# The last two tiles reach the router unnormed, their logits corrected afterwards; buffers and steps without a pair put in another order

## The reference

```python
x = x + memory_attention(layernorm(x))          # 8 kv heads; elu(q)+1 times M, over a denominator, then Wo
x = x + cross_attention(layernorm(x), ctx)      # below
x = x + router_ffn(layernorm(x))                # below
# cross_attention: 32 query heads in 4 groups, keys and values from concat(ctx, latents)
q = (latents @ Wq).reshape(b, q_len, 4, 8, 128)
attn = softmax(einsum('bqhgd,bkhd->bhgqk', q, k) * scale)
out = einsum('bhgqk,bkhd->bqhgd', attn, v).reshape(b, q_len, 4096) @ Wo
# router_ffn: 64 experts, 8 kept
logits = flat @ router_weight.T + router_bias
scores = softmax(logits)
topk_w, topk_idx = lax.top_k(scores, 8)
out = flat * topk_w.sum(-1) + w_dense @ expert_bias
```

## Time and profile before

| | before |
|---|---|
| median of 3 runs | 720.72 us (719.7 to 722.87) |
| the profiled execution's own time | 720.87 us |
| its span, first to last instruction | 719.1 us |
| PE busy | 692.9 us, 96% |
| DVE, ACT, POOL busy | 510.3, 349.5, 115.8 us |
| mean granted PE clock | 0.993 of full speed |

### The profile page before, as it was taken

How to read it: one execution, slowest core, us unless ns; L and a number is a source line. 1 busy time by engine, 2 the same in 40 slices (tenths; PEclk the granted TensorE clock), 3 DMA queues, 4 the chain that set the end, 5 groups by cost and what they waited for, 6 DMA issues and landing times.

```text
span 719.1 us, 10998 instructions
## 1 busy us (share of the span) xinstructions
PE 692.9 (96%) x3562; PEld 581.1 (81%) x3562; DVE 510.3 (71%) x1078; ACT 349.5 (49%) x1042; POOL 115.8 (16%) x121
## 2 busy tenths in 40 slices
PE   8999699999999998999999999999999999899995
PEld 6888588887887787888888888888888888688874
DVE  2764877678725878677677876767977566778876
ACT  4454655456244446344445643554645336555541
POOL 0175400000101332020120220210202000022410
PEclk9999999999999999999999999999999999999998
DMA  9888510001234456543242833423542404221101
GB/s 329 296 288 286 205 59 1 1 0 59 88 118 143 135 170 206 189 147 100 77 126 80 263 102 102 146 87 110 194 146 78 146 31 154 75 82 59 59 16 58
DMA packets 69997, 90.14 MB, mean 125 GB/s; under 512 B 4224, under 2 KB 47232, under 8 KB 69952
## 3 DMA queue, kind: packets, MB, share of 16 engines
q1 hardware_dynamic: 64160, 80.13, 34.2%
q10 hardware_dynamic: 5792, 9.44, 3.7%
HBM read 62.29 MB, written 27.26 MB: 125 GB/s over the span
## 4 chain that ended last, share of the span: by engine, by line
PE 83%; DVE 8%; DMA 2%; issue 2%; ACT 2%; POOL 1%; SPq 0%; POOLq 0%; ACTq 0%; DVEq 0%
PE bank L896 23%; PE bank L828 19%; PE bank L652 14%; PE bank L965 7%; PE bank L1014 5%; PE bank L798 5%; PE bank L991 4%; PE bank L643 1%; DMA raw<-in_L_attn_Wo 1%; PE bank L765 1%; DVE regA L1364 1%; PE bank L687 1%; PE bank L731 1%; DVE forms L1364 1%; DMA raw<-in_ctx 1%
## 5 line engine op out<-in xcount | busy, mean ns | idle before, releaser
L896 PE MATMUL bank<-regA,oT 128*128 128x512 f32 x768 | 180.6, 391 | 3.1 <-DVE oT L1364 3.1
L896 PEld LDWEIGHTS bank<-regA,oT 128*128 128x128 f32 x768 | 143.4, 188 | 33.3 <-DVE oT L1364 3.9
L1290 ACT ACTIVATE probs<-bank,negmax 128x128 f32<-128x128 f32 x256 | 90.1, 378 | 46.0 <-DVE negmax L1741 46.0
L828 PE MATMUL bank<-xnT,forms 128*128 128x512 f32 x384 | 97.2, 397 | 0.2
L828 PEld LDWEIGHTS bank<-xnT,forms 128*128 128x128 f32 x384 | 70.1, 188 | 15.2 <-DVE qbuf L1571 1.7
L828 PE MATMUL bank<-regC,forms 128*128 128x512 f32 x288 | 75.8, 401 | 2.4 <-DVE qbuf L1571 2.4
L1044 ACT CAST oT<-bank 128x512 fp32r<-128x512 f32 x64 | 37.6, 588 | 79.3 <-PE bank L1014 76.5
L1044 ACT CAST pT<-bank 128x512 fp32r<-128x512 f32 x64 | 34.7, 592 | 69.5 <-PE bank L991 69.5
L652 PE MATMUL bank<-regC,xnT 128*128 128x512 f32 x256 | 67.8, 396 | 0.0
L965 PEld LDWEIGHTS bank<-k_ring,qbuf 128*128 128x128 f32 x512 | 62.0, 191 | 2.5
L828 PEld LDWEIGHTS bank<-regC,forms 128*128 128x128 f32 x288 | 52.8, 190 | 12.9 <-DVE qbuf L1571 2.4
(11 more groups left out here) (151 smaller groups left out, 1072.0 us busy)
## 6 DMA issues: line engine op xcount, KB each, us to landing
q_dram<-qbuf SPq DMA_DIRECT2D x32, 512.0 KB, 3.0
qbuf<-q_dram SPq DMA_DIRECT2D x31, 512.0 KB, 4.5
raw<-in_L_attn_Wo SPq DMA_DIRECT2D x8, 1024.0 KB, 7.6
raw<-in_L_xattn_Wo SPq DMA_DIRECT2D x4, 2048.0 KB, 9.9
wq_raw<-in_L_xattn_Wq SPq DMA_DIRECT2D x16, 512.0 KB, 4.1
k_ring<-keys_dram SPq DMA_DIRECT2D x32, 128.0 KB, 3.6
v_raw<-vals_dram SPq DMA_DIRECT2D x64, 64.0 KB, 3.5
rawk<-in_L_xattn_Wv SPq DMA_DIRECT2D x4, 512.0 KB, 4.0
```

The source lines that it names most:

```text
L828: last = nc.tensor.matmul(k_bank[:, :], forms[:, p[1], a, i, c, :], right(b)[:, c, :], start=j == 0, stop=j == 5)
L896: last = nc.tensor.matmul(bank[7][:, :], oT[:, a, h, :], wo[:, b, h, :], start=h == 0 and i == 0, stop=h == GH - 1 and i == 2)
L1290: last = nc.scalar.activation(probs[:, bb, p, :], bank[bb][:, p * P:(p + 1) * P], ACT.Exp, bias=negmax[:, bb, p:p + 1], accum_out=rowsum[: ...
```

## The change

It has these parts:

- **Staging buffers.** `kv_slots` is turned round, so result 14 lies in `qneg` and result 15 in `kvout`. ACT's first exp then waits for result 14's write; DVE waits for result 15's only ahead of the first denominator sum.
- **End of the memory attention.** The transposes of latent tile 5 and DVE's and ACT's share in them move one step back; the split of the key weights (`wkv_high(1, ...)`, `wkv_low(1, ...)`) moves behind the last latent tile.
- **Last forms before the steps.** `summed_high` and `summed_low` of pair 5 move from ahead of step (0,0) into it.
- **Steps without a pair.** In (2,7) and (3,1) the last two heads of `project` come behind the transposes of the probabilities. At a group's first step ACT makes its last four `wo_high` ahead of the rounding of `oT`. In step (3,0) DVE makes two `wo_low` ahead of `oT` and two behind it, and POOL makes the last four.
- **Router.** A matrix of ones times the router's weights gives their sums once (`router_sums`, four matmuls in step (3,2)). Tiles 6 and 7 are transposed as raw residual; DVE corrects the logits by mean and rstd, kept by `keep_norm`. The last mix has its own bank, the tail's streams are reordered.

```diff
-        kv_slots = (qneg[:, :], qb[:, :], kvout[:, :])
+        kv_slots = (kvout[:, :], qb[:, :], qneg[:, :])
...
+        def mix_bank(e):
+            return bank[0] if e == NT - 1 else bank[2]
+
+        def rows_of(e):
+
+            return resid[:, e, :] if e >= NT - 2 else e_xn_of(e)
...
+            pool.wait_ge(form_lo, 4 * PAIRS)
+            nc.gpsimd.memset(ones, 1.0).then_inc(ones_set, 1)
+            for h in range(4, GH):
+                pool.wait_ge(wo_hi, GH * (KV - 1) + h + 1)
+                pool.wait_ge(wo_lo, GH * (KV - 1) + h)
+                nc.gpsimd.tensor_tensor(wo[:, 1, h, :], wo_raw[:, h, :], wo[:, 0, h, :].bitcast(F), ALU.subtract)\
+                    .then_inc(wo_lo, 1)
...
-                if output_in(i):
+                if output_in(i) and i != 2 * NT + 1:
                     latent_transposes(output_in(i) - 1)
+                if i == 2 * NT + 2:
+                    latent_transposes(output_in(i - 1) - 1)
...
             def expert_transposes(e):
-                pe.wait_ge(e_xn_ready, e + 1)
+                if e >= NT - 2:
+                    pe.wait_ge(proj_added, 8 * (KV - 1) + e + 2)
+                else:
+                    pe.wait_ge(e_xn_ready, e + 1)
...
+            def router_sums():
+
+                pe.wait_ge(routT_ready, 1)
+                pe.wait_ge(ones_set, 1)
+                for c in range(KC):
+                    nc.tensor.matmul(bank[3][:, NE:2 * NE], ones, routT[:, c, :], start=c == 0, stop=c == KC - 1)
...
+                divided = not pair and not (last_group and t >= 2) and t
+                front = range(GH - 2) if divided else range(GH)
                 if not first_step:
                     if t == 0:
                         project(g - 1, 7, True)
                     else:
-                        project(g, t - 1, False)
+                        project(g, t - 1, False, front)
...
+                elif divided:
+                    project(g, t - 1, False, range(GH - 2, GH))
...
+            expert_transposes(NT - 2)
             project(KV - 1, NT - 1, False)
-            expert_transposes(NT - 2)
+            expert_logits(NT - 2)
             expert_weights(NT - 3)
+            expert_transposes(NT - 1)
             expert_mix(NT - 3)
-            expert_logits(NT - 2)
-            expert_transposes(NT - 1)
             expert_logits(NT - 1)
...
-            act.wait_ge(kv_written[0], kv_count(0, 16))
+            act.wait_ge(kv_written[2], kv_count(2, 16))
...
             for p in range(LEAD + 1):
                 copy_1(p)
-                summed_high(p + 1, (p + 1) % 2)
+                if p < LEAD:
+                    summed_high(p + 1, (p + 1) % 2)
...
-                if t % 2 and has_pair(g, t + 2):
+                if first_step or t % 2 and has_pair(g, t + 2):
                     summed_high(pair + 1, slot)
...
+                    if s == 0:
+                        dve.wait_ge(kv_written[0], kv_count(0, 16))
...
             x_low(tr("latent", NT - 1), NT - 1)
+            wkv_low(1, wkv2, 3 * KC, 0)
...
+            def keep_norm(e):
+
+                r = e % 2
+                nc.vector.tensor_copy(top[:, r, 1, 1:2], meanvar[:, 0:1])
+                settled(nc.vector.tensor_scalar(top[:, r, 1, 2:3], rstd[:, 0:1], -1.0, None, ALU.mult))
+
...
+                if e == 0:
+                    nc.vector.tensor_copy(rout_sums, bank[3][:, NE:2 * NE])
+                if e < NT - 2:
+                    nc.vector.tensor_tensor(logits, bank[3][:, 0:NE], rout_b, ALU.add).then_inc(logits_saved, 1)
+                    dve.wait_ge(logits_saved, e + 1)
+                else:
+
+                    nc.vector.scalar_tensor_tensor(out=small[:, r, 4, :], in0=rout_sums, scalar=top[:, r, 1, 1:2],
+                                                   in1=bank[3][:, 0:NE], op0=ALU.mult, op1=ALU.subtract)\
+                        .then_inc(logits_saved, 1)
+                    dve.wait_ge(logits_saved, e + 1)
+                    settled(nc.vector.scalar_tensor_tensor(out=logits, in0=small[:, r, 4, :],
+                                                           scalar=top[:, r, 1, 2:3], in1=rout_b,
+                                                           op0=ALU.mult, op1=ALU.add))
...
-                if t % 2 and has_pair(g, t + 2):
+                if first_step or t % 2 and has_pair(g, t + 2):
                     summed_low(p + 1, slot)
...
                 if t == 0 and not first_step:
-                    for h in range(2 if p is not None else 0, 4):
+                    for h in range(2) if p is None else range(2, 4):
                         wo_low(g, h)
...
                 if t == 0 and not first_step:
-                    for h in range(4, GH):
+                    for h in range(2, 4) if p is None else range(4, GH):
                         wo_low(g, h)
```

More of the change, by code:

```diff
@@ L885, in _, with project @@
                 product_3(pair)
-            def project(g, t, release):
+            def project(g, t, release, heads=range(GH)):
                 n = 8 * g + t
-                pe.wait_ge(oT_lo, 2 * n + 2)
-                pe.wait_ge(proj_added, n + 1)
-                for h in range(GH):
+                if heads[0] == 0:
+                    pe.wait_ge(oT_lo, 2 * n + 2)
+                    pe.wait_ge(proj_added, n + 1)
+                for h in heads:
                     if t == 0:
@@ L1316, in step @@
                     high(pT[:, bb, 0, :], bank[bb][:, :]).then_inc(pT_hi, 1)
+                if t == 0 and not first_step:
+                    act.wait_ge(proj_done, 8 * g)
+                    for h in range(4, GH):
+                        wo_high(g, h)
                 for bb in range(2):
@@ L1821, in _ @@
                 step(KV - 1, t, True)
+            expert_rows(NT - 2)
+            keep_norm(NT - 2)
             add_mix(NT - 4)
@@ L1827, in _ @@
             expert_moments(NT - 1)
+            expert_max(NT - 2)
             expert_rows(NT - 1)
[L1829 removed]
+            keep_norm(NT - 1)
             add_mix(NT - 3)
```

46 lines of the change are left out of this document (21 added, 25 removed).

## The result

The changed kernel takes 735.77 us (median of 4 runs, 733.65 to 738.87) against 720.34 of before in the same runs: a ratio of 1.0205, 95% interval 1.0164 to 1.0246. It is 15 us slower, where 7.7 were forecast. The profiled execution took 735.96 us, with a span of 734.2.

The account below looks back on a forecast made before the run. PE's stream was taken to bound the kernel, busy 692.9 of 719.1 us. Terms summed to -4.7, giving 725.4 us; two clock falls (-3.0) made the forecast 728.4 us, range 720.0 to 731.5.

Parts of the forecast that it names:

- the latent value products hide it: End of the memory attention: the late key weights' split serves only the latent key products, so costs nothing; unhidden, 2.8 us.
- the clock fall at the first step: Behind the new wait for `qbuf` at the scores of (0,1): PE's clock falls, 1.5 us lost.
- End of the memory attention, +0.6: Tile 6's norm on DVE comes one operation earlier, PE waits less: 0.6 us gained, bounds +0.3 and +0.6.
- Pair 5, -1.6 and 1.5 of clock: Step (0,0): old wait and clock fall go, but `qbuf` loads late: 1.6 us lost, plus 1.5 for a new fall.
- `wo_low` on POOL, -5.2 and 1.5: Steps (3,0), (3,1): POOL's four subtractions delay the router's loads: 5.2 us lost, plus 1.5 for a clock fall.
- Heads in (2,7), +1.0: Step (2,7): heads 6 and 7 behind the transposes fill PE's idle 1.01 us ahead of L1014: 1.0 us gained.
- router: Step (3,2): four more f32 matmuls for the sums, partly filling small waits: 0.3 us lost, bounds 0 and -0.9.
- tail: Kernel's end: transposes fill a wait, the last mix skips DVE's add: 0.6 us gained, bounds +0.3 and +1.1.
- Staging buffers, +0.2: Memory steps: ACT and DVE start earlier, but POOL's folds hold DVE: 0.2 us gained, bounds -0.2 to +0.85.
- Clock: Behind the two new waits of 5 and 6 us: one clock fall each, 1.5 us apiece, 3.0 us lost.
- The fifth rival: Worse than forecast: POOL and DVE hold each other up much longer, over 731.5 us; chance 0.05.

Follow-up runs that it names:

- wkv_back: Changed kernel with the split of the key weights at its old place, ahead of tile 5's rounding; 731.54 us, ratio to before 1.0155.
- wkv_alone: The kernel undivided with only the key weights' split at the late place the change gives it; 721.69 us, ratio to before 1.0003.
- save_first: Changed kernel with ACT's rounding of pair 0's summed forms one copy later, behind the last latent value tile's copy; 728.8 us, ratio to before 1.0107.
- changed_again: The changed kernel, word for word, run again beside the others on one chip; 736.49 us, ratio to before 1.0223.
- wo_back: Changed kernel with POOL's four `wo_low` given back to DVE, which makes all eight; 727.61 us, ratio to before 1.0116.
- q_first: Changed kernel with SP's loads of `k_ring` (tile 3) and `qbuf` (step (0,1)) ahead of its wait and `load_pair(6)`; 726.05 us, ratio to before 1.0067.
- mended: Changed kernel with q_first's load order, the wkv split and `wo_low` back, (3,1) in one piece; pair 5 stays in step (0,0); 717.71 us, ratio to before 0.996.
- three_back: Changed kernel with the wkv split, POOL's `wo_low` and pair 5's forms all put back; 721.5 us, ratio to before 1.0021.
- pool_early: The kernel undivided with POOL making four `wo_low`, DVE's four all ahead of `oT`; 722.87 us, ratio to before 1.0034.
- undivided: three_back with the projection of step (3,1) in one piece again, (2,7) still divided; 717.67 us, ratio to before 0.9953.
- slots_back: The kernel undivided with `kv_slots` and ACT's and DVE's waits for the writes as before; 716.59 us, ratio to before 0.9944.
- pair_back: Changed kernel with `summed_high` and `summed_low` of pair 5 ahead of step (0,0) again; 729.68 us, ratio to before 1.0135.

## Why the prediction was off

**Step that failed: of the wkv split, "the latent value products hide it".** The prediction put the term at nothing: I priced the late place by who uses the split's result, and found that they come later. I did not ask what stands behind it on DVE's queue. That is the 4.5 us at 203, shown by wkv_back, wkv_alone (4.3) and, with the exact link, save_first (0.2 left). Of the 7.4 us that the median lies above the forecast this is over half. A second term was too small, the clock fall at the first step, below. The 3.3 us near 245 were not forecast either; they hang on how long one weight load took in the profiled execution, and changed_again does not have them.

All profiles, matched with before's (us later, -: earlier):

| place | profiles with the part as in the change | with it undone |
|---|---|---|
| latent values and keys | +4.3 to +4.5 in five, +2.9 in wo_back | 0.0 in six, +0.2 in save_first |
| scores of (0,0) to (0,2) | +2.7 in the changed trace, +4.1 to +4.3 in four | -1.0 to 0.0 in six; -3.0 in q_first and mended |
| scores of (3,0) to (3,2) | +6.5 to +7.7 in six | +2.5 in wo_back and three_back, +3.3 in pool_early, 0.0 in four |

**End of the memory attention, +0.6.** The size is right: 0.6 us in all profiles with the late wkv split. But it comes from the split being out of the way; with the split back (wkv_back, three_back, undivided and others: 0.0) the tile's new order only moves PE's wait. A gain of this term is not there by itself.

**Pair 5, -1.6 and 1.5 of clock.** The mechanism was right to the link: issue 0.97 us behind the weight load's, landing after 5.1 us (5.7 forecast), a wait of 4.0 us (5 forecast). q_first shows that it is the queue. The sum of the two, 3.1, is 2.7 in the changed trace and 4.1 to 4.3 in four others: what was under-sized is the clock fall behind the new wait, 1.6 us in the first and 2.7 to 2.9 in the others where 1.5 were forecast. Besides, the term is credited with the clock fall of before, and this fall is not there in every execution.

**`wo_low` on POOL, -5.2 and 1.5.** The total came right, 6.8 us in the trace for 6.7, but in part by luck. POOL's four took 6.1 us (5.4 and 1.1 forecast), and the issue and L928 came where they were forecast. I gave the whole to the late loads. With POOL's four back on DVE, 2.5 us stay (wo_back, three_back), and they go only with (3,1) in one piece (undivided), so the late loads account for 4.3. In the prediction that division had a price only behind the late loads; that it takes 1.4 us of work from in front of a wait was missed. How much the division costs while POOL is late was not tried.

**Heads in (2,7), +1.0, router, tail.** +1.3, -0.1 and +0.6 in the trace; right. **Staging buffers, +0.2.** Not to be told from nothing; slots_back agrees.

**Clock.** I forecast two falls of 1.5 us. The changed trace has five ahead of its tail, before has one. Summed over windows of 2 us, PE's busy time multiplied by the share of the clock that is missing is 8.7 us up to the tail, against 1.7 in before; with the tails it is 9.5 against 2.5. The difference, 7 us, is about the 6.6 us by which PE's busy time rose.

**The working.** Two small slips change nothing in it: 633.4 less 628.09 is 5.3 lost and not 5.2, and the bounds at their worse ends add up to -7.1 and not -7.3. The measured 735.8 us lies above the high end either way. The fifth rival had a time above 731.5 us, but by POOL and DVE holding each other up for much longer, and they did not: POOL's four took 6.1 us where 6.5 were forecast.

What stays open: by medians the parts undone one at a time give back 4.4, 8.3 and 6.3 us, 19.0 together, but all three at once 14.5. With intervals of 4.2, 2.2 and 2.9 us to either side, four runs each, that gap is not clear of noise; at their places in the traces the three come to 12 to 15 us. And the unprofiled runs can't be looked into, neither for the 245 wait nor for their clock falls by place.

## What to carry to other kernels

An instruction that is moved late must be priced by everything behind it on its own queue, and by what the next engine has queued behind the wait for it, not by the readers of its result alone; and by the idle time in front of it, if its own input comes late there (2.55 us here). The same holds for a load behind a semaphore wait on the issuing queue: four of the 15 us were one wait placed in front of two loads that had nothing to do with it. And an idle gap filled by taking work from in front of another wait is only moved.

## What the runs showed of the hardware

The same wait has two prices. PE waits 1.8 to 2.0 us at the first step in seven profiles. In before, three_back and slots_back the clock falls behind it; in undivided, pair_back, pool_early and wkv_alone it stays at 1.00. Windows of undivided and then of three_back behind it:

```profile
272.00:274.00 2.00, 1.51 (x7) 1.14 (x8) 1.82 (x4) 2.00 (x13) 0.00 (x0) 1.00 0.83 249
```

```profile
272.00:274.00 2.00, 2.00 (x8) 1.48 (x8) 1.56 (x5) 1.79 (x11) 0.00 (x0) 0.74 1.07 376
274.00:276.00 2.00, 2.00 (x9) 1.65 (x9) 1.98 (x4) 0.95 (x2) 0.00 (x0) 0.50 0.67 231
```

At 1.00 in the one, 0.74 and 0.50 in the other. The waits of these two are the same within 0.01 us (1.88), so whether the clock falls does not follow from the length alone. L669's wait of 2.62 us says the same: behind it the clock fell in five profiles and stayed at 1.00 in wo_back, where the place cost 2.9 us and not 4.3 to 4.5. In before even 2.86 us at 83 had no fall. Behind waits of 4 us and more it fell every time: at the scores of (0,1) (five profiles, 4.0 to 4.4 us), at L928 (six, 5.1 to 5.5 us) and at L748 (pair_back 5.5, mended 5.0 us).

A fall cost 1.7 us in the changed trace at 206 (2 x 0.49 + 2 x 0.36) and 2.8 at 284 in changed_again (three windows at 0.50, 0.50 and 0.62), so my 1.5 us was below both. This can be one reason why executions of one kernel spread over several us here: each wait near 2 us either has a fall or has not. Another can be PE's waits for the low parts of Wo in the memory steps, 1.8 to 6.1 us in all over the profiles; a third is the landing of a pair's weight load, 3.7 to 5.4 us, with the wait of 0 to 1.9 us that hangs on it. How the spread divides among them is not shown.
